# Later list and chain steps in the attention, a third stage for the expert tiles, and five PSUM banks for the last attention steps

## The reference

```python
q = _rope((x @ Wq.T + bq).reshape(B, L, H, Dh), sin, cos); k = _rope(...); v = ...
attn = softmax(einsum('bqhd,bkhd->bhqk', q, k) / sqrt(Dh), axis=-1)
x = _layernorm(x + einsum('bhqk,bkhd->bqhd', attn, v).reshape(B, L, D) @ Wo.T + bo)

def _moe_group(x2, router_w, wg, wu, wd, top_k):     # 8192 rows, 32 experts, top_k = 2
    scores = softmax(x2 @ router_w)
    expert_weights, expert_indices = lax.top_k(scores, top_k)
    # rows sorted by expert, one grouped product after another, scatter-add by row
    ys = ragged_dot(silu(ragged_dot(xs, wg, sizes)) * ragged_dot(xs, wu, sizes), wd, sizes)
    return zeros_like(x2).at[tok].add(ys * flat_w[order][:, None])

x = _layernorm(x + (out0 * 2 + out1 * 2) / 4)
```

## Time and profile before

| | |
|---|---|
| runs, median of 3 | 2554.54 us (2549.39 to 2559.07) |
| profiled execution | 2565.6 us, of which span 2563.8 us |
| mean granted TensorE clock | 0.942 |
| busy PE / PEld / DVE / ACT / POOL | 2299.0 / 1154.4 / 1788.1 / 1608.9 / 1040.8 us |
| attention (8 batches, second pass from 108.1) | to about 1819 us |
| batches' second pass starts at | 108.1, 300.8, 511.5, 730.2, 950.7, 1169.2, 1387.8, 1606.6 us |
| first gate/up product, last silu | 1827.6, 2528.0 us |
| DMA moved | 371.29 MB |

### The profile page before, as it was taken

The page is one execution under the profiler, slowest core; times in us unless marked ns, Lnnn a source line. Parts: engine busy times, 40 slices in busy tenths (PEclk is TensorE's granted clock), DMA queues, the critical chain, the costliest instruction groups (busy, mean ns, idle before and its releaser), DMA issues.

```text
span 2563.8 us, 44333 instructions
## 1 busy us (share of the span) xinstructions
PE 2299.0 (90%) x12529; PEld 1154.4 (45%) x12537; DVE 1788.1 (70%) x3364; ACT 1608.9 (63%) x3613; POOL 1040.8 (41%) x886
## 2 busy tenths in 40 slices
PE   5999999998999989999998999988797989999884
PEld 3433333433433333343343334333475767776663
DVE  4888878889778878877878887883145423346766
ACT  1277777776766867776676776767343434565654
POOL 3121240334435345343434535242456455554442
PEclk6599999999989999999999999998698999999997
DMA  6223532444433544443454335553554465689986
GB/s 171 75 63 81 130 88 47 127 110 113 131 105 86 154 125 103 117 134 106 108 142 127 87 111 155 154 175 111 143 174 148 149 206 195 228 250 290 286 284 202
DMA packets 210346, 371.29 MB, mean 145 GB/s; under 512 B 32512, under 2 KB 150016, under 8 KB 205888
## 3 DMA queue, kind: packets, MB, share of 16 engines
q1 hardware_dynamic: 181784, 291.46, 41.4%
q0 software_dynamic: 27552, 75.40, 8.1%
q10 hardware_dynamic: 776, 1.59, 0.3%
HBM read 204.84 MB, written 135.69 MB: 133 GB/s over the span
## 4 chain that ended last, share of the span: by engine, by line
PE 61%; DVE 20%; issue 6%; DMA 5%; ACT 3%; SPq 3%; POOL 1%; another core or an unknown queue 1%; ACTq 0%; DVEq 0%; POOLq 0%
PE ps_a L902 17%; PE ps_o L920 15%; DVE maxima_sb L1137 12%; PE ps_a L1661 8%; PE ps_b L823 5%; PE ps_b L892 4%; PE ps_b L1681 4%; PE ps_b L833 3%; PE ps_a L1648 2%; ACT probs_sb L770 2%; DMA back_sb<-y_dram 1%; DVE w_gu_sb L1980 1%; PE ps_b L1670 1%; SPq L1420 1%; DVE stats_sb L1011 1%
## 5 line engine op out<-in xcount | busy, mean ns | idle before, releaser
L1137 DVE TENSOR_REDUCE maxima_sb<-ps_a 128x1 f32<-128x1024 f32 x1024 | 1226.7, 1219 | 298.5 <-PE ps_a L902 274.4
L770 ACT ACTIVATE probs_sb<-ps_b 128x512 f32<-128x512 f32 x2048 | 1094.2, 599 | 420.4 <-PE ps_b L892 401.5
L902 PE MATMUL ps_a<-k_stack_sb,q_stack_sb 48*128 48x512 f32 x2048 | 740.7, 459 | 88.2 <-DVE maxima_sb L1137 60.2
L892 PE MATMUL ps_b<-q_stack_sb,k_stack_sb 50*128 50x512 f32 x2048 | 781.0, 464 | 17.8 <-ACT probs_sb L770 8.9
L902 PEld LDWEIGHTS ps_a<-k_stack_sb,q_stack_sb 48*128 48x128 f32 x2048 | 316.8, 193 | 682.5 <-DVE maxima_sb L1137 375.8
L920 PE MATMUL ps_o<-probs_sb,v_sb_sb 128*32 128x512 f32 x4096 | 562.7, 622 | 14.6 <-ACT o_raw_sb L778 14.1
L1518 POOL DMA_INDIRECT y_dram<-y_rows_sb,spot_sb x318 | 314.8, 990 | 328.5 <-ACT y_rows_sb L1583 294.4
L1661 PE MATMUL ps_a<-w_gu_sb,x_cols_sb 128*128 x1272 | 359.5, 407 | 23.2 <-issue 10.4
L892 PEld LDWEIGHTS ps_b<-q_stack_sb,k_stack_sb 50*128 50x128 f32 x2048 | 322.6, 189 | 118.1 <-ACT probs_sb L770 83.2
L170 POOL DMA_INDIRECT rows_dram<-stage_sb,listed_sb x208 | 201.7, 970 | 277.4 <-PE ps_o L920 243.9
L1661 PEld LDWEIGHTS ps_a<-w_gu_sb,x_cols_sb 128*128 128x128 f32 x1272 | 225.1, 197 | 78.3 <-issue 53.2
(11 more groups left out here) (230 smaller groups left out, 2035.5 us busy)
## 6 DMA issues: line engine op xcount, KB each, us to landing
x_rows_sb<-rows_dram SPq DMA_DIRECT2D x318, 128.5 KB
back_sb<-y_dram SPq DMA_DIRECT2D x80, 256.0 KB
parts_dram<-parts_q_sb SPq DMA_DIRECT2D x16, 1024.0 KB
parts_dram<-parts_k_sb SPq DMA_DIRECT2D x16, 1024.0 KB
w_gu_sb<-w_gu SPq DMA_DIRECT2D x16, 1024.0 KB, 4.2
swapped_sb<-feat_qk_sb SPq DMA_DIRECT2D x62, 256.0 KB
q_stack_sb<-parts_dram SPq DMA_DIRECT2D x62, 256.0 KB
k_stack_sb<-parts_dram SPq DMA_DIRECT2D x62, 256.0 KB
```

The lines of the kernel that those rows point to most:

```text
L770: act.activation(probs[t % NPR][:, j, :], src[:, :], ACT.Exp, scale=float(DH) ** -0.5).then_inc(s_bdrain, 1)
L892: pe.matmul(out[:, :], k_stack[u % NSTK][lo:lo + XROWS, jj, kc * P:(kc + 1) * P].bitcast(F32R), q_stack[u % NSTK][lo:lo + XROWS, jj, qh * ...
L902: ins = pe.matmul(out[:, kh, :], q_stack[u % NSTK][lo:lo + ROWS, jj, qt * P:(qt + 1) * P].bitcast(F32R), k_stack[u % NSTK][lo:lo + ROWS, j ...
L1137: vec.tensor_reduce(maxima[u % 2][:, 1 - k, i:i + 1], src[:, :, :].rearrange("p a q -> p (a q)"), AX.X, ALU.max).then_inc(s_adrain, 1)
```

## The change

It has four parts.

1. For the first six batches `norm` begins 7 steps earlier with one statistics instruction in a step, each waiting only for its own projection; `scale` begins 5 steps earlier with one tile in a step over eight steps; `choices` comes 2 steps earlier. In `top2` the 16 MAX_INDEX stand ahead of the subtraction `shifted`, which so comes four steps later. The list scatters of tiles 6 and 7 of the first five batches' lists move from steps 51 to 58 to steps 62 to 69.
2. ACT's copy of `ps_o` stands between the second and the third exponential of its step.
3. In the last 22 steps the second pass uses a ring of five banks: the three of `ps_b` and the two halves of `ps_a[0]`. What else wants a `ps_a` tile there has `ps_a[1]` alone.
4. The expert tiles have three gate/up banks (the third is `ps_b[2]`) and three buffers `gate` and `hidden`; the transpose of `hidden` runs two tiles behind and the down product three. The down product has only the bank `ps_b[1]` for tiles 0 to 69 and `ps_b[1]` and `ps_o` from tile 70 on. Two steps of the tail (`FIRST_AT`, `LAST_AT`) are one slot later.

The new functions `b_place` and `a_place` give the bank of a tile and which earlier use of it is to be waited for.

```diff
     end = SPB * (b + 1)
     if b < nb - 2:
-        at = dict(O=22, norm=30, scale=43, T=48, L=50, x1=48, top2=55, exp=67, route=68, choose=69, marks=72, R=76, ranks=77,
-                  rank_sums=78, choices=84)
+        at = dict(O=22, norm=23, scale=38, T=48, L=50, x1=48, top2=55, exp=67, route=68, choose=69, marks=72, R=76, ranks=77,
+                  rank_sums=78, choices=82)
         rate = 1
     else:
         at = dict(O=22, norm=30, scale=40, T=42, L=43, x1=42, top2=45, exp=47, route=48, choose=48, marks=49, R=50, ranks=51,
...
 def list_at(nb, b, t):
 
     if b < nb - 3:
-        return SPB * (b + 2) + 27 + LISTS * t, 1
+        return SPB * (b + 2) + (27 if t < KC - 2 else 38) + LISTS * t, 1
     if b == nb - 3:
         return SPB * (b + 2) + 23 + LISTS * t // 2, 2
...
-FIRST_AT, LAST_AT, ADD_LAG = 8, 6, 4
+FIRST_AT, LAST_AT, ADD_LAG = 9, 7, 4
 AHEAD = 8
+NGU, HT_LAG, DOWN_LAG = 3, 2, 3
+TWO_Y = OWNER_AT[1] + 4
...
+            b_lone, a_lone = nb_all, na_all
...
+        lone_ring = [ps_b[(b_lone + i) % NBR] for i in range(NBR)] + [ps_a[0][:, i, :] for i in range(2)]
+
+        def b_place(n):
+
+            if n < b_lone:
+                return ps_b[n % NBR], n - NBR, None
+            i = n - b_lone
+            if i < NBR:
+                return lone_ring[i], n - NBR, None
+            if i < len(lone_ring):
+                return lone_ring[i], None, max(a for a in range(a_lone) if a % NAR == 0)
+            return lone_ring[i % len(lone_ring)], n - len(lone_ring), None
+
+        def a_place(n):
+
+            if n < a_lone:
+                return ps_a[n % NAR], n - NAR
+            return ps_a[1], n - 1 if n > a_lone else max(a for a in range(a_lone) if a % NAR == 1)
...
-                if 0 <= t < n_steps:
-                    for j in heads_of(t):
-                        src = arrived()
-                        if t >= NPR:
-                            act.wait_ge(s_pv, t - NPR + 1)
-                        act.activation(probs[t % NPR][:, j, :], src[:, :], ACT.Exp,
-                                       scale=float(DH) ** -0.5).then_inc(s_bdrain, 1)
-                n = t - PV_LAG
-                if 0 <= n < n_steps and n % KC == KC - 1:
-                    done = n // KC
-                    act.wait_ge(s_pv, n + 1)
-                    if done >= 2 and done % 2 == 0:
-                        act.wait_ge(s_oraw, 16 * (G + 1) * (done // 2))
-                    act.activation(o_raw[:, done % 2, :], ps_o[:, :], ACT.Copy).then_inc(s_ocp, 1)
+                for k in range(2):
+                    if 0 <= t < n_steps:
+                        for j in heads_of(t)[2 * k:2 * k + 2]:
+                            src = arrived()
+                            if t >= NPR:
+                                act.wait_ge(s_pv, t - NPR + 1)
+                            act.activation(probs[t % NPR][:, j, :], src[:, :], ACT.Exp,
+                                           scale=float(DH) ** -0.5).then_inc(s_bdrain, 1)
+                    n = t - PV_LAG
+                    if k == 0 and 0 <= n < n_steps and n % KC == KC - 1:
+                        done = n // KC
+                        act.wait_ge(s_pv, n + 1)
+                        if done >= 2 and done % 2 == 0:
+                            act.wait_ge(s_oraw, 16 * (G + 1) * (done // 2))
+                        act.activation(o_raw[:, done % 2, :], ps_o[:, :], ACT.Copy).then_inc(s_ocp, 1)
...
-                    i, n = t - at["scale"], 2 * at["rate"]
+                    i, n = t - at["scale"], 1 if at["rate"] == 1 else 4
...
-                if n >= NBR:
-                    pe.wait_ge(s_bdrain, n - NBR + 1)
-                return ps_b[n % NBR]
+                bank, b_last, a_last = b_place(n)
+                if a_last is not None:
+                    pe.wait_ge(s_adrain, a_last + 1)
+                elif b_last >= 0:
+                    pe.wait_ge(s_bdrain, b_last + 1)
+                return bank
...
-                vec.wait_ge(s_adrain, a_no[("O", b, KC - 1)] + 1)
                 for i in range(KC):
+                    vec.wait_ge(s_adrain, a_no[("O", b, i if chain_at(nb, b)["rate"] == 1 else KC - 1)] + 1)
                     vec.bn_stats(stats[:, i, :], y[:, i, :]).then_inc(s_norm, 1)
-                    yield 3
+                    yield 4
                 vec.wait_ge(s_norm, at + KC)
...
+                for i in range(n):
+                    vec.max_index(top_idx[:, i, :], top_val[:, i, :], logits[:, i, :]).then_inc(s_top, 1)
+                    yield 1
                 vec.tensor_tensor(shifted[:, 0:n * NE].rearrange("p (a e) -> p a e", e=NE), logits[:, :, :],
                                   top_val[:, :, 0:1].to_broadcast([P, n, NE]), ALU.subtract).then_inc(s_top, 1)
                 yield 6
                 vec.tensor_tensor(shifted[:, n * NE:], top_val[:, :, 1], top_val[:, :, 0], ALU.subtract).then_inc(s_top, 1)
                 yield 1
-                for i in range(n):
-                    vec.max_index(top_idx[:, i, :], top_val[:, i, :], logits[:, i, :]).then_inc(s_top, 1)
-                    yield 1
...
-        ps_g = [ps_a[1][:, i, :] for i in range(2)]
-        ps_h, ps_y, ps_id = ps_b[0], ps_b[1:3], ps_o
+        ps_g = [ps_a[1][:, 0, :], ps_a[1][:, 1, :], ps_b[2]]
+        ps_h, ps_y, ps_id = ps_b[0], [ps_b[1], ps_o], ps_o
+        y_bank = lambda m: ps_y[m % 2 if m >= TWO_Y else 0]
...
-                if n - 1 > 0:
-                    act.wait_ge(s_hid, n - 1)
-                act.activation(gate[n % 2][:, :], ps_g[n % 2][:, 0:HID], ACT.Silu).then_inc(s_silu, 1)
+                if n >= NGU:
+                    act.wait_ge(s_hid, n - NGU + 1)
+                act.activation(gate[n % NGU][:, :], ps_g[n % NGU][:, 0:HID], ACT.Silu).then_inc(s_silu, 1)
...
-                if HT_FROM < n <= N:
-                    hidden_columns(n - 1)
-                if 2 <= n < N + 2:
-                    rows_out(n - 2)
+                if HT_FROM <= n - HT_LAG < N:
+                    hidden_columns(n - HT_LAG)
+                if 0 <= n - DOWN_LAG < N:
+                    rows_out(n - DOWN_LAG)
...
-                if n - 1 > 0:
-                    pe.wait_ge(s_yr, n - 1)
-                pe.matmul(ps_y[n % 2][:, 0:D], hidden_t[n % 2][:, :], w_d[:, bass.ds(e * D + down_at(g), D)],
+                if n == TWO_Y + 1:
+                    pe.wait_ge(s_cdrain, len(c_no))
+                elif n > 0:
+                    pe.wait_ge(s_yr, n if n <= TWO_Y else n - 1)
+                pe.matmul(y_bank(n)[:, 0:D], hidden_t[n % 2][:, :], w_d[:, bass.ds(e * D + down_at(g), D)],
...
-            for n in range(N + 2):
+            for n in range(N + DOWN_LAG):
-                if 1 <= n <= N:
-                    transpose_h(n - 1)
-                if 2 <= n:
-                    down(n - 2, expert.pop(n - 2))
+                if 0 <= n - HT_LAG < N:
+                    transpose_h(n - HT_LAG)
+                if 0 <= n - DOWN_LAG:
+                    down(n - DOWN_LAG, expert.pop(n - DOWN_LAG))
```

38 lines of the change are left out of this document (20 added, 18 removed).

## The result

| | before | after |
|---|---|---|
| median of 4 runs | 2551.97 us (2544.96 to 2559.07) | 2484.49 us (2478.41 to 2490.95) |
| ratio, 95% interval | | 0.9723 (0.9684 to 0.9762) |
| profiled execution, span | 2565.6, 2563.8 us | 2489.8, 2488.0 us |
| mean granted clock | 0.942 | 0.957 |
| first silu, last silu, end of span | 1828.7, 2528.0, 2563.8 | 1749.1, 2451.2, 2488.0 |

The account below looks back on a forecast made before the run. Attention was taken as a PE, ACT and DVE ring stopped at batch ends by scatter blocks, the tiles as paced by PE's waits. 45 + 5 + 6 + 36 = 92 us off 2565.6, less 11.1, gave 2462; range 2415 to 2522.

Parts of the forecast that it names:

- Lists and subtraction: Batch ends in attention: later scatters cut the interval to 30 us, 39 us; the later subtraction adds 2 in batch 1.
- The subtraction at its new place: DVE at step 63: may wait for list scatters, at worst 0.97 us in each of five batches, 5 us.
- The rest of the chain: Norm, scale and choices in the first batches: less work put into one step, 4 us for six batches.
- The copy: ACT's copy of `ps_o` in every eighth attention step comes two exponentials earlier: 5 us, ends 0 and 14.
- Five banks: Last 22 attention steps: PE runs further ahead of ACT, 6 us at the start of the tiles, ends 0 and 10.
- The third stage: Expert tiles: one more tile of time for each product cuts PE's waits for `hidden`, 36 us taken.
- Rival B: Expert tiles: bound elsewhere, by DMA or DVE; they give 8 instead of 36 us, 2490; chance 0.20.
- The single bank for y: Expert tiles up to tile 69: down product waits for ACT's copy of the tile before; set at 0.
- Rival C: Attention and tiles: waits fed on one another; clock nears 0.98, interval becomes 27.6 us, 2422 in all; chance 0.10.
- Rival A: Batch ends: the block of scatters isn't the cause, or scatters stay late; 12 instead of 45 us, 2495; chance 0.14.

Follow-up runs that it names:

- the opened block: The kernel before, the eight list scatters of tiles 6 and 7 in their old place, nine small POOL memsets behind each: 2520.57 us, ratio 0.9854.
- the run meant for it: The kernel before with three small POOL memsets behind each of the eight list scatters of tiles 6 and 7: 2465.73 against 2462.77 us, ratio 1.0005.

## Why the prediction was right and wrong

The range (2415 to 2522) held 2484.49, the sign was right, and the forecast of 2462 was 22 us too low. That it came so near is partly luck, as two errors of opposite sign made up for each other. Up to the first silu 56 us were forecast (45 + 5 + 6) and 79.6 measured, 4.2 of them chance; for the tiles 36 were forecast and none came. By its steps, from the two profiled executions, which are 75.8 us apart:

- *Lists and subtraction.* Forecast 39 + 2 with a new interval of 30 us. Measured: 222.6 us in the six intervals before, 6 × 27.6 = 165.6 after, 57.0 us. The mechanism was right, shown by the opened block and by the lists alone; the size was too small, because I set the interval by DVE's extra work of MAX and MAX_INDEX, and that costs nothing beyond the step. Of the 10.2 us of batch 3, 7.5 are the block (37.8 to 30.3) and 2.7 the subtraction and the small one behind it.
- *The subtraction at its new place* was allowed up to 0.97 us of waiting for scatters, and it has none: 670 to 675 ns in all seven. In the attention it fell between two scatters, so those seven don't test the price. The subtraction of the last batch, which stands among the tiles, does; it started inside an indirect DMA and took no longer:

```profile
1840.34 0.96 POOL L1548 DMA_INDIRECT y_dram<-y_rows_sb,spot_sb  x1 [1.48 <-ACT y_rows_sb L1613]
1841.12 0.68 DVE L1868 TENSOR_TENSOR shifted_sb<-logits_sb,top_val_sb 128x512 f32<-128x512 f32 x1
```

  The rule of the Trainium skill, "SBUF — State Buffer", section "🔬 SBUF: two separate sides", on a VectorE instruction with two SBUF inputs beside a GpSimd instruction that reads SBUF, agrees with POOL's arithmetic (2.77 us beside line 392 in the run of the lists alone, 0.67 without). No run here shows an indirect DMA that holds up the subtraction.
- *The rest of the chain.* Forecast 4. The intervals three to five of a batch, 26.9, 23.2 and 28.3 us in the run with the copy alone, are 26.4, 22.8 and 27.2 in the changed kernel, 2.1 us a batch, 13 in six. That is by exclusion, as the chain's steps were not run alone. Against it stand the second intervals: over batches 1 to 6 they are 150.8 us in sum with the copy alone and 158.2 in the profile after (153.3 to 166.7 in the five profiles with the changed chain, single ones from 24.3 to 30.6). So some of the 13 is lost again, and what lengthens them is open.
- *The copy.* Forecast 5, measured alone 7.
- *Five banks.* Forecast 6, measured alone 6. In the profile after the last batch is 13.7 us shorter from step 10 on, but the first silu comes 10.4 us later behind it; PE waits there for rows that a DMA reads back from the lists (15.58 us, to 1744.86). 3.3 are left. The mechanism, that the lists of batch 6 bound what the tiles can see of it, fits.
- *The third stage.* Forecast 36, measured −2.9 in the profile, −2 (−7 to +4) alone, and none on the third chip (643.2 with it, 642.8 and 647.9 without). This is the step that failed: "One more stage gives each product one tile more, 1.71 us, so it can take away nearly all of that, 30 × 1.71 = 51 us, if no other wait takes its place." The wait for `hidden` was booked on DVE's product, and why the product was late wasn't asked. The trace of the kernel before has two reasons.

  Behind 12 of the 30 waits, 24.0 of the 51.9 us, the silu started 1.2 to 6.0 us after its product had ended and ACT was free, like the one at 2024.62 above. There a signal was late. Seven of these stops are longer than a tile's 1.71 us, and in the rows above several engines stop at once, so one stage more couldn't cover them; this last is argued, not shown. Two further waits, 7.6 us, have ACT late for another reason.

  Behind the other 16, 20.3 us and 13 of them in the second group of experts, the silu was on time. DVE was late, as it executes in order and had other work ahead, in the second group the combination of finished rows. In six of the 16 it stood there itself for over 1 us until a DMA had read the rows back, as here:

```profile
2406.26 0.28 ACT L1577 ACTIVATE gate_sb<-ps_a 128x128 f32<-128x128 f32 x1 [0.68 <-PE ps_a L1661]
2409.02 1.01 DVE L1980 SCALAR_TENSOR_TENSOR w_gu_sb<-back_sb,weight_sb,w_gu_sb 128x256 f32<-128x256 f32 x2 [3.96 <-DMA back_sb<-y_dram]
2410.01 0.28 DVE L1956 TENSOR_TENSOR hidden_sb<-gate_sb,ps_a 128x128 f32<-128x128 f32 x1
2410.34 0.14 PEld L1670 LDWEIGHTS ps_b<-consts_sb,hidden_sb 128*128 128x128 f32 x1 [2.89 <-DVE hidden_sb L1956]
```

  Late signals can't be the whole reason: on the third chip, which has none, PE still waits 36.1 to 42.5 us for `hidden`, 27 to 33 us of it behind DVE in the same way, and the stage gives nothing there either. With the stage the wait went from 30 pieces to 40 and didn't shrink. Rival B (0.20) said that the tiles would give 8 instead of 36, since DMA or DVE bound them; for the last stretch (DMA share 0.88 at 276 GB/s, DVE waiting for rows read back) it fits what the traces show, but no run tested it. Why the stage gained nothing against the waits behind DVE stays open.
- *The single bank for y* cost nothing: the wait of the down product for the copy of y is 3.5 us in the page's row against 0.5 us of all waits before.
- Rival C had the new interval right, 27.6 us, and the clock wrong: in the first tiles it is 0.88 where it was 0.87, and they take 167.3 us instead of 168.
- Rival A, that the block is not the cause, fell on the chip on which the block was opened. Its point "a scatter is only 0.97 us of POOL" was beside the matter: the opened block holds POOL longer and costs less.

The parts sum up: 4.2 us by the start of the first batch (between 125.4 and 138.5 us at the first copy over fourteen profiles of nearly the same code, so chance), 57.0 in the interval behind step 56, 15.3 in the other intervals to batch 7, 3.3 to the first silu, −2.9 in the tiles and −1.0 behind them, together 75.9, 0.1 off by rounding.

What stays open: why signals are late beside unbroken scatters on two or three chips and not on another, and how far apart is enough between 1.28 and 3.02 us, as the run meant for it fell on the chip without the stop.
